# Products of a constant on TensorE, written to unused PSUM banks, at the beginning and at two joints of a six-stage decoder kernel

## The chip, the cores and the metric

The kernel runs on one core of one Trainium2 chip. The metric is the device time of one execution in microseconds (us). A core has five engines with queues of their own: TensorE (matrix products, shown as PE, its weight loads as PEld), VectorE (DVE), ScalarE (ACT), GpSimd (POOL) and SyncE (SP), which issues the DMAs here. They wait for each other by semaphores. TensorE writes only to PSUM, which has eight banks. TensorE's clock has two levels, 1.2 and 2.4 GHz; the profile shows which one was granted, as 0.50 and 1.00 of full speed.

## The reference

Two decoder layers over 32 sequences of 128 tokens with 256 features, all in float32. Each layer is self-attention, cross-attention and a feed-forward part, each with a layer norm before it and a residual add behind it:

```python
    x = x + _L0_attn_ref(_layernorm(x, axis=-1), L0_attn_Wqkv, L0_attn_bqkv, L0_attn_Wout, L0_attn_bout)
    x = x + _L0_xattn_ref(_layernorm(x, axis=-1), ctx_1024, L0_xattn_Wq, L0_xattn_bq, L0_xattn_Wk, L0_xattn_bk, L0_xattn_Wv, L0_xattn_bv, L0_xattn_We, L0_xattn_be)
    x = x + _L0_ffn_ref(_layernorm(x, axis=-1), L0_ffn_gate_W, L0_ffn_gate_b, L0_ffn_wi_W, L0_ffn_wi_b, L0_ffn_wo_W, L0_ffn_wo_b, L0_ffn_lora_A, L0_ffn_lora_B)
    x = x + _L1_attn_ref(_layernorm(x, axis=-1), L1_attn_W_query, L1_attn_W_key, L1_attn_W_val, L1_attn_W_out)
    x = x + _L1_xattn_ref(_layernorm(x, axis=-1), ctx_1024, ctx_1024, mask_SxS2_bk0, L1_xattn_wq, L1_xattn_bq, L1_xattn_wk, L1_xattn_bk, L1_xattn_wv, L1_xattn_bv, L1_xattn_wo, L1_xattn_bo)
    x = x + _L1_ffn_ref(_layernorm(x, axis=-1), L1_ffn_W_fc, L1_ffn_ln_w, L1_ffn_ln_b, L1_ffn_W_proj)
    return x
```

The first part is rotary attention with 16 heads of 16 features. The second mixes queries and keys of the context in one tanh layer and attends with one head. The third chooses one of eight experts for a token and adds its low-rank term (rank 4) to a shared feed-forward of 1024. The change touches the first three parts only.

## The kernel before

The activations (`x_res`) stay in SBUF for the whole kernel. The 32 sequences are worked on in 16 pairs (`NG` = 16 groups of `TOK` = 256 tokens). Each of the six parts is a stage, and each stage is a block of instructions for every engine: a0, b0, c0, a1, a2, d1. In the trace their tiles are called a_ (all three attention stages), b_, c_ and d_, and those shared by stages all_. A stage begins on an engine when all engines have ended the stage before.

In a stage the groups are pipelined in software: the order of each engine's instructions is written out by hand as a loop over windows, the first and last few unrolled. A window holds, for TensorE, steps of several groups. To keep float32 accuracy, most products run as three passes (`three_pass`, line 104: high part by high part, low by high, high by low) over operands that ScalarE rounds to a high part and from which VectorE or GpSimd takes the low part.

The places that matter here:

- **Beginning of stage a0.** SyncE loads the activations and weights. VectorE makes the constants (`Constants.prepare`; `ones` is one of them, line 129), normalises group 0 (`all_xn`), TensorE turns it (line 206, `a_FB<-all_ident,all_xn`), then waits until the weights are split (`all_odd_split`, line 298) and projects the queries (`a_FA`), the keys (`a_FB`) and the values (`a_FA`), then the value bias (line 1164). VectorE takes them out (`a_q`, line 901) and adds the bias of the values (line 996); with that the scores start (line 1010).
- **End of a0.** The last products are the output projection `a_FA` (line 104). VectorE adds it to `x_res` and splits the last of the next stage's weights (`all_even_split`, line 471). The score banks are `S1_0`, `S1_1`, `S2_0`, `S2_1`.
- **Beginning of b0.** ScalarE and GpSimd make the high and low part of the context (`b_cT_hi`, line 234; `b_cT_lo`, line 238). TensorE waits for both, then `b_ENT` has 24 products.
- **End of b0.** In the last window TensorE makes the last scores (`b_SC`, line 1444), waits for their exponentials (`b_probs`, line 1369, after two steps of VectorE), turns them (`b_PP`, line 1470) and multiplies with the values (`b_OUT`, line 1484).
- **Beginning of c0.** The gate (`c_RT`, 40 columns wide, line 104) is followed by the choice of the expert on VectorE (lines 1602 to 1611), and TensorE waits for its result `c_low_parts` before it turns it (`c_LT`, line 1692) and starts the hidden layer (`c_HB`, lines 1671 to 1674).

The order in the window of c0 at the place of the last edit is:

```python
                elif in_stage(w + 1):
                    gate(w + 1, 1 - parity)
                if in_stage(w - 1):
                    pe.wait_ge(hlo_ok, w * HALVES)
...
                if in_stage(w + 1):
                    pe.wait_ge(low_ok, w + 2)
```

Of the kernel before, what the change touches and what calls it, by code (L numbers as in the profile page):

```python
# [21 lines left out]
P = 128  # L22
# [4 lines left out]
NG = NB // PAIR  # L27
# [80 lines left out]
class Constants:  # L108


    def __init__(self, nm, a):
        self.from_dram = {k: a[k] for k in ("ident", "head_mask", "turn_sign")}
        self.tiles = {
            "ident": nm.sb("ident", [P, P]), "head_mask": nm.sb("head_mask", [P, HV]), "turn_sign": nm.sb("turn_sign", [P, 1]),
            "ones": nm.sb("ones", [P, P]), "minus_half": nm.sb("minus_half", [P, PAIR]), "minus_one": nm.sb("minus_one", [P, PAIR]), "ln_eps": nm.sb("ln_eps", [P, PAIR]),
            "ident_b": nm.sb("ident_b", [P, P], BF16), "neg_ident_b": nm.sb("neg_ident_b", [P, P], BF16),
        }
        self.loaded, self.ready = nm.sem("consts_loaded"), nm.sem("consts_ready")

    def load(self, sp):  # L120
        for k, src in self.from_dram.items():
# [2 lines left out]
    def prepare(self, dve):  # L124
        tiles = self.tiles
        dve.memset(tiles["minus_half"][:], -0.5)
        dve.memset(tiles["minus_one"][:], -1.0)
        dve.memset(tiles["ln_eps"][:], LN_EPS)
        dve.memset(tiles["ones"][:], 1.0)
        dve.wait_ge(self.loaded, 16 * len(self.from_dram))  # L130
        dve.tensor_copy(tiles["ident_b"][:], tiles["ident"][:])
        dve.tensor_scalar(tiles["neg_ident_b"][:], tiles["ident"][:], -1.0, None, ALU.mult).then_inc(self.ready, 1)


class GroupNorm:
# [434 lines left out]
def attention_stage(nc, name, before, norm, next_norm, consts, wt, following, spare, context=None, next_context=None, mask_dram=None,  # L570
# [90 lines left out]
    def has_window(G):  # L661
        return not isinstance(G, int) or G + 1 < NG
# [33 lines left out]
    with nc.Block() as block:  # L696
# [307 lines left out]
        def _(pe):  # L1004
# [176 lines left out]
            def group(G, parity):  # L1181
                for t in range(0, STEPS, 2):
                    if vo_bias and t == 0 and isinstance(G, int) and G == 0:
                        pe.wait_ge(vo_added, PAIR)
                    scores(G, t, parity)
                    if cross and has_step(G, t):
                        mask_step(G, t)
                        mask_step(G, t + 1)
                    if has_step(G, t - 2):
                        shift_step(G, t - 2)  # L1190
                        shift_step(G, t - 1)
                    if t in (0, 4) and whole(G - 1):
                        turn((G - 1) * PAIR + t // 4, t // 4)
                    if t in (2, 6) and whole(G - 1):
                        turn_back((G - 1) * PAIR + t // 4, t // 4)
                    if t == 0 and whole(G - 2):
                        output(G - 2)
                    if t == 0:
                        transposes(G)
                    if t == 2 and has_window(G):  # L1200
                        queries(G, parity)
                    if t == 4 and has_window(G):
                        keys(G)
                    if t == 6 and has_window(G):
                        values(G)
                    if vo_bias and t == 6 and isinstance(G, int) and G < 0:
                        value_bias()
                    if t == 6 and isinstance(G, int) and G == NG:
                        output(G - 1)
                    if t in (2, 6) and has_step(G, t - 6):  # L1210
                        for u in range(NQ):
                            av_step(G, t - 6 + u, parity)
                    if isinstance(G, int) and G >= following.first:
                        free = ((next_norm.lo_ok, 1), (max_ok, NG * STEPS)) if G + 1 >= NG else ((q_free, q_reads * (G + 2)),)
                        for u in range(2):
                            following.pe_slot(pe, (G - following.first) * STEPS + t + u, next_banks(G), free)
            if x_dram is not None:
                pe.wait_ge(constants.ready, 1)
            schedule(pe, group)
    nm.end()  # L1220
    return nm

# [71 lines left out]
def starts(w):  # L1294

    return isinstance(w, int) and w == 0
# [12 lines left out]
def in_stage(w):  # L1309
    return not isinstance(w, int) or 0 <= w < NG  # L1310


def entangled_stage(nc, name, before, norm, next_norm, consts, context, wt, following):
# [23 lines left out]
    with nc.Block() as block:  # L1337
# [99 lines left out]
        def _(pe):  # L1437
            def window(w, parity):
                if in_stage(w - 1):
                    pe.wait_ge(vt_ok, w)  # L1440
                    at_least(pe, exp_ok, w - 1)
                    for b in range(PAIR):
                        for k in range(KC):
                            last = pe.matmul(SC[:, b * P:(b + 1) * P], ent[:, k, b * P:(b + 1) * P],
                                             vT[:, k, b * P:(b + 1) * P], start=(k == 0), stop=(k == KC - 1))
                    last.then_inc(sc_full, 1)
                if not starts(w):
                    ln.pe_transpose(pe, w)
                if in_stage(w):
                    hi, lo, chi, clo = ln.hi[parity], ln.lo[parity], cT_hi[parity], cT_lo[parity]  # L1450
                    if isinstance(w, int) and w == 0:
                        pe.wait_ge(wt.w_ok, 3)
                    pe.wait_ge(ln.lo_ok, w + 1)
                    pe.wait_ge(c_lo, w + 1)
                    at_least(pe, ent_ok, w)
# [43 lines left out]
def routed_stage(nc, name, before, norm, next_norm, consts, wt, following):  # L1499
# [32 lines left out]
    with nc.Block() as block:  # L1532
# [109 lines left out]
        def _(pe):  # L1642
# [12 lines left out]
            def window(w, parity):  # L1655
# [19 lines left out]
                        last.then_inc(hb_full, 1)  # L1675
                elif in_stage(w + 1):
                    gate(w + 1, 1 - parity)
                if in_stage(w - 1):
                    pe.wait_ge(hlo_ok, w * HALVES)
                    at_least(pe, out_ok, w - 1)  # L1680
# [405 lines left out]
```

## Time and profile before

| | |
|---|---|
| median of 3 runs | 1392.95 us (1390.52 to 1396.66) |
| profiled execution, its time | 1392.18 us |
| its span (first to last instruction) | 1390.1 us |
| TensorE busy | 1318.4 us (95%) |
| mean granted clock of TensorE | 0.986 |
| VectorE, ScalarE, GpSimd busy | 71%, 53%, 33% |

The profile was taken from one execution. Its times start at the first instruction. An engine is busy while an instruction of it runs. A busy TensorE may run at either clock, so its busy time alone does not tell how fast it works.

### The profile page before, as it was taken

To read this page: it belongs to the slowest core of one execution; us is meant where nothing else is said; L and a number is where in the kernel's file an instruction comes from. 1 tells how busy PE (TensorE), PEld (TensorE's weight loads), DVE (VectorE), ACT (ScalarE), POOL (GpSimd) and SP (SyncE) were. 2 spreads that over 40 slices of the span, in tenths; PEclk is the share of its full clock that TensorE was granted. 3 is DMA by queue.
4 is the path that set the end of the run, shared out by engine and by line. 5 is a ranking of instruction groups with operands and counts; after the bars stand their busy time and mean duration, and the time that the engine had idled before them with its cause. 6 is when DMAs were issued, how large, how long until landed. Compare 5 with 4: busy or idle time off the path is not lost. (4 is left out here: it accounts for less than half of the span.)

```text
span 1390.1 us, 41799 instructions
## 1 busy us (share of the span) xinstructions
PE 1318.4 (95%) x15764; PEld 1192.3 (86%) x15764; DVE 987.4 (71%) x2431; ACT 732.8 (53%) x1469; POOL 455.0 (33%) x550
## 2 busy tenths in 40 slices
PE   5999999889978999999999999979999999899997
PEld 5899989789968999999899899868888888689997
DVE  5888888556655554554777778767777778768885
ACT  3655555445554544543556556535555556456562
POOL 2212221122221121210000000036555556478884
PEclk9999999999998999999999999999999999999999
DMA  6000000031100000000100000020000000000000
GB/s 233 2 2 0 0 0 2 2 113 38 38 4 28 2 0 0 0 0 3 54 2 0 0 0 1 2 78 17 17 15 15 15 15 2 2 24 23 30 31 31
DMA packets 16622, 29.26 MB, mean 21 GB/s; under 512 B 3632, under 2 KB 7728, under 8 KB 16144
## 3 DMA queue, kind: packets, MB, share of 16 engines
q1 hardware_dynamic: 16528, 27.97, 6.1%
q8 instruction: 64, 1.05, 0.3%
q14 instruction: 30, 0.25, 0.1%
HBM read 23.77 MB, written 4.19 MB: 20 GB/s over the span
## 5 line engine op out<-in xcount | busy, mean ns | idle before, releaser
L883 DVE TENSOR_REDUCE a_row_max<-a_S 128x4 bf16<-128x512 f32 (+1 forms) x384 | 247.1, 684 | 51.0 <-PE a_S L1051 25.5
L776 ACT ACTIVATE a_probs<-a_S 128x512 f32<-128x512 f32 x384 | 209.1, 595 | 117.2 <-PE a_S L1064 60.1
L175 POOL TENSOR_TENSOR all_var_eps<-all_moments,all_ln_eps 128x2 f32<-128x2 f32 x96 | 25.0, 260 | 604.8 <-DVE all_moments L170 604.8
L1019 PE MATMUL a_S<-a_qm_hi,all_odd_split 32*128 32x256 f32 x1536 | 188.5, 303 | 7.4 <-DVE a_row_max L883 5.6
L738 POOL TENSOR_TENSOR a_shifts<-a_add_mask,a_row_max 128x512 bf16<-128x512 bf16 x128 | 135.1, 1071 | 117.1 <-DVE a_row_max L883 117.1
L1019 PEld LDWEIGHTS a_S<-a_qm_hi,all_odd_split 32*128 32x128 f32 x1536 | 132.3, 184 | 41.8 <-issue 26.6
L1010 PE MATMUL a_S<-all_odd_split,a_qm_hi 32*128 32x128 f32 x1536 | 127.8, 285 | 1.7 <-DVE all_odd_weights L996 1.7
L1019 PE MATMUL a_S<-a_qm_lo,all_odd_split 32*128 32x256 f32 x768 | 108.8, 277 | 0.0
L1077 PE MATMUL a_AV<-a_probs,a_v_pad 128*32 128x128 f32 x3072 | 103.8, 276 | 0.0
L1010 PEld LDWEIGHTS a_S<-all_odd_split,a_qm_hi 32*128 32x128 f32 x1536 | 100.7, 186 | 2.7 <-DVE all_odd_weights L996 2.5
L781 ACT ACTIVATE a_av_raw<-a_AV 128x512 f32<-128x512 f32 x96 | 57.6, 600 | 77.0 <-PE a_AV L1077 76.1
L198 DVE TENSOR_SCALAR all_xn<-all_x_res,all_moments,all_rstd 128x256 f32 (+1 forms) x164 | 85.3, 561 | 14.1 <-POOL all_rstd L177 13.3
L104 PE MATMUL c_OUT<-all_odd_split,c_h_hi 128*128 128x256 f32 x512 | 90.3, 277 | 0.9 <-DVE all_x_res L1635 0.9
L1077 PEld LDWEIGHTS a_AV<-a_probs,a_v_pad 128*32 128x32 f32 x3072 | 78.0, 109 | 13.1 <-issue 1.5
L1769 POOL TENSOR_TENSOR d_scaled_hid<-d_hid,all_odd_weights 128x512 f32<-128x512 f32 x64 | 81.5, 1293 | 7.3 <-ACT d_hid L1801 6.3
L104 PE MATMUL a_FA<-all_odd_split 128*128 128x256 f32 x576 | 80.5, 289 | 2.0 <-DVE all_odd_split L896 1.9
L1566 ACT ACTIVATE c_h<-c_HB,all_odd_weights 128x256 f32<-128x256 f32 x128 | 53.8, 472 | 50.0 <-PE c_HB L1674 48.9
L1064 PE MATMUL a_S<-all_neg_ident_b,a_row_max 128*128 128x128 bf16 x1024 | 79.8, 221 | 0.0
L104 PEld LDWEIGHTS c_OUT<-all_odd_split,c_h_hi 128*128 128x128 f32 x512 | 78.5, 188 | 1.0 <-issue 1.0
L896 DVE TENSOR_TENSOR all_odd_split<-a_AV,all_odd_split 128x256 fp32r<-128x256 f32 x96 | 40.7, 424 | 51.3 <-ACT all_odd_split L786 50.4
L177 POOL TENSOR_TENSOR all_rstd<-all_var_eps,all_minus_half 128x2 f32<-128x2 f32 x96 | 73.2, 762 | 7.5
L104 PEld LDWEIGHTS a_FA<-all_odd_split 128*128 128x128 f32 x576 | 71.7, 190 | 2.6 <-DVE all_odd_split L896 2.3
(260 smaller groups left out, 3835.1 us busy)
## 6 DMA issues: line engine op xcount, KB each, us to landing
all_x_res<-in_x SPq DMA_DIRECT2D x8, 512.0 KB, 8.1
all_cx<-in_ctx_turned SPq DMA_DIRECT2D x16, 256.0 KB, 2.8
all_cx<-in_ctx SPq DMA_DIRECT2D x16, 256.0 KB, 2.8
out_x<-all_x_res SPq DMA_DIRECT2D x16, 256.0 KB, 2.0
b_routed_wi<-in_L_ffn_wi_W SPq DMA_DIRECT2D x1, 1024.0 KB, 5.1
b_routed_wo<-in_L_ffn_wo_W SPq DMA_DIRECT2D x1, 1024.0 KB, 7.4
all_even_weights<-in_L_ffn_W_fc SPq DMA_DIRECT2D x1, 1024.0 KB, 5.1
all_even_weights<-in_L_ffn_W_proj SPq DMA_DIRECT2D x1, 1024.0 KB, 6.9
```

The source lines that it names most:

```text
L104: last = pe.matmul(out, w(k), m(k), start=(k == 0 and n == 0), stop=(k == chunks - 1 and n == 2))
L177: pool.tensor_tensor(self.rstd[:], self.var_eps[:], self.minus_half[:], ALU.pow).then_inc(self.rstd_ok, 1)
L198: last = dve.tensor_scalar(self.xn[:, b, :], self.x(w, b), self.moments[:, b, 0:1], self.rstd[:, b:b + 1], ALU.subtract, ALU.mult)
L738: pool.tensor_tensor(shifts[:, t % 4], add_mask[:], row_max[:, t % 4, :].rearrange("p (h o) -> p h o", o=1).to_broadcast([P, QH, P]), ALU. ...
L776: act.activation(probs[:, t % STEPS, :], S2[t % 2][:], ACT.Exp, scale=DH ** -0.5).then_inc(exp_ok, 1)
L781: act.activation(av_raw[:], AV[b][:], ACT.Copy).then_inc(raw_ok, 1)
L883: dve.tensor_reduce(row_max[:, t % 4, :], S1[t % 2][:].rearrange("p (h k) -> p h k", h=QH), AXX, ALU.max).then_inc(max_ok, 1)
L1010: return pe.matmul(S1[t % 2][:, at * P:(at + 1) * P], qm_hi[parity][strip, c, b, v, :], k_hi[parity][strip, c, tok], start=(not cross or a ...
L1019: pe.matmul(S2[t % 2][:, c * HV * P:(c + 1) * HV * P], k[par][strip, c, tok], q[par][strip, c, b].rearrange("p h t -> p (h t)"), start=(c ...
L1064: last = pe.matmul(part, row_max[:, t % 4, h:h + 1].to_broadcast([P, P]), neg_ident_b[:], start=False, stop=h == QH - 1, skip_group_check= ...
L1077: last = pe.matmul(AV[b][32 * h:32 * h + 32, j * P:(j + 1) * P], v_pad[par][:, b, j * QH + h, :], probs[:, t % STEPS, h * P:(h + 1) * P], ...
L1769: pool.tensor_tensor(half_of(scaled_hid[parity], n), half_of(hid[parity], n), gain_row[:, half * HB_COLS:(half + 1) * HB_COLS], ALU.mult). ...
```

## The change

A helper `fill` issues a number of float32 products of the 128x128 tile of ones with itself, all to the first 128 columns of a PSUM bank that nothing is using at that point; nobody reads the result. It is called at six places in the code, and six groups of products come of it: 20 before the first wait for the constants, 18 behind the first transposes, 10 at the end of stage a0, 8 at the beginning of b0 before its first products, 14 in the last window of b0 and 10 behind the first gate of c0. A new semaphore tells TensorE that the ones are written.

```diff
-        self.loaded, self.ready = nm.sem("consts_loaded"), nm.sem("consts_ready")
+        self.loaded, self.ready, self.ones_ok = nm.sem("consts_loaded"), nm.sem("consts_ready"), nm.sem("ones_ok")
...
-        dve.memset(tiles["ones"][:], 1.0)
+        dve.memset(tiles["ones"][:], 1.0).then_inc(self.ones_ok, 1)
...
+def fill(pe, consts, bank, n):
+
+    for _ in range(n):
+        pe.matmul(bank[:, 0:P], consts["ones"][:], consts["ones"][:], start=True, stop=True, skip_group_check=True)
...
                     if t == 2 and has_window(G):
+                        if x_dram is not None and isinstance(G, int) and G < 0:
+                            fill(pe, consts, S2[0], 18)
                         queries(G, parity)
...
             if x_dram is not None:
+                pe.wait_ge(constants.ones_ok, 1)
+                fill(pe, consts, S2[0], 20)
                 pe.wait_ge(constants.ready, 1)
             schedule(pe, group)
+            if x_dram is not None:
+                fill(pe, consts, S2[0], 10)
...
+                if isinstance(w, int) and w == NG:
+                    fill(pe, consts, VT, 14)
                 if not starts(w):
                     ln.pe_transpose(pe, w)
...
                     if isinstance(w, int) and w == 0:
                         pe.wait_ge(wt.w_ok, 3)
+                        fill(pe, consts, VTOK, 8)
                     pe.wait_ge(ln.lo_ok, w + 1)
...
                 elif in_stage(w + 1):
                     gate(w + 1, 1 - parity)
+                    fill(pe, consts, OUT, 10)
```

TensorE's queue at the start of the kernel, first as it was (a_FB takes the turned group 0, a_FA the queries):

```order
L1003 UNCONDITIONAL_BRANCH
L206 MATMUL a_FB<-all_ident,all_xn 128x128 x4
L104 MATMUL a_FA<-all_xT_hi,all_odd_split 128x256 x2
L104 MATMUL a_FA<-all_xT_lo,all_odd_split 128x256
L104 MATMUL a_FA<-all_xT_hi,all_odd_split 128x256 x2
```

and as it is in the changed kernel (its lines are numbered a little higher):

```order
L1009 UNCONDITIONAL_BRANCH
L138 MATMUL a_S_0<-all_ones 128x128 x20
L212 MATMUL a_FB<-all_ident,all_xn 128x128 x4
L138 MATMUL a_S_0<-all_ones 128x128 x18
L104 MATMUL a_FA<-all_xT_hi,all_odd_split 128x256 x2
L104 MATMUL a_FA<-all_xT_lo,all_odd_split 128x256
```

Both groups stand ahead of instructions that wait, so these can start only when the products of ones are through. TensorE's queue across the end of b0 and the start of c0 (the two branches are the stage's end and start), in the changed kernel:

```order
L1506 MATMUL b_VTOK<-all_ident,b_vT 128x128 x4
L1456 MATMUL b_SC<-b_vT,b_ent 128x128 x4
L138 MATMUL b_VT<-all_ones 128x128 x14
L1485 MATMUL b_PP<-all_ident,b_probs 128x128 x2
L1499 MATMUL b_OUT<-b_v_tok,b_probsT 128x256 x2
L1349 UNCONDITIONAL_BRANCH
L1656 UNCONDITIONAL_BRANCH
L104 MATMUL c_RT<-all_odd_split,all_xT_hi 128x40
...
L138 MATMUL c_OUT<-all_ones 128x128 x10
L1708 MATMUL c_LT<-all_ident,c_low_parts 96x128 x2
L212 MATMUL c_PT<-all_ident,all_xn 128x128 x4
```

Before, the same rows stood there without the two of line 138. Nothing else moved, on TensorE or on another engine.

## Rows read from the trace of the kernel before

**Rows 1.** The page: TensorE's busy time and the granted clock in 40 slices

```profile
PE 1318.4 (95%) x15764; PEld 1192.3 (86%) x15764; DVE 987.4 (71%) x2431; ACT 732.8 (53%) x1469; POOL 455.0 (33%) x550
...
PEclk9999999999998999999999999999999999999999
```

**Rows 2.** TensorE by stretch: length, busy (records), granted clock, DMA share, GB/s

```profile
14.67:18.63 3.96, 3.93 (x18) 1.00 1.02 415
18.63:25.46 6.83, 5.23 (x40) 1.00 1.03 358
25.46:32.28 6.82, 6.78 (x60) 0.50 0.06 20
282.32:288.28 5.96, 5.93 (x28) 0.50 0.97 382
411.16:424.82 13.66, 9.17 (x37) 0.50 0.26 79
420.56:424.82 4.26, 4.26 (x20) 0.50 0.01 4
435.06:438.47 3.41, 3.41 (x18) 0.50 0.00 0
```

**Rows 3.** Timeline at a0's end and b0's start: start, us, engine, instruction [idle before]

```profile
275.64 1.70 PE L104 MATMUL a_FA<-all_odd_split 128*128 128x256 f32 x12 [0.93 <-DVE all_odd_split L896]
...
279.25 0.68 DVE L471 TENSOR_TENSOR all_even_split<-all_even_weights,all_even_split 128x512 fp32r<-128x512 f32 x1
...
280.94 1.26 POOL L238 TENSOR_TENSOR b_cT_lo<-all_cx,b_cT_hi 128x512 fp32r<-128x512 f32 x1 [21.60 <-ACT b_cT_hi L234]
...
282.35 0.77 PE L104 MATMUL b_ENT<-all_xT_hi,all_even_split 128*128 128x256 f32 x2 [5.01 <-POOL b_cT_lo L238]
```

**Rows 4.** Waits of TensorE: us in total, times, longest

```profile
PE a_FB L206 <- DVE all_xn L198: 8.7, 1, 8.7
...
PE c_LT L1692 <- DVE c_low_parts L1611: 4.7, 2, 2.6
```

**Rows 5.** Timeline at the beginning of a0

```profile
0.94 0.17 DVE L129 MEMSET all_ones<- 128x128 f32 x1
...
8.65 1.09 PE L206 MATMUL a_FB<-all_ident,all_xn 128*128 128x128 f32 x4 [8.65 <-DVE all_xn L198]
...
14.70 0.77 PE L104 MATMUL a_FA<-all_xT_hi,all_odd_split 128*128 128x256 f32 x2 [4.96 <-DVE all_odd_split L298]
...
17.71 0.88 DVE L901 SCALAR_TENSOR_TENSOR a_q<-a_FA,all_odd_weights 128x256 f32<-128x256 f32 x2 [1.95 <-PE a_FA L104]
...
22.65 0.75 DVE L996 TENSOR_TENSOR all_odd_weights<-all_odd_weights,a_S 128x256 f32<-128x256 f32 x2 [0.34 <-PE a_S L1164]
...
23.46 0.66 PE L1010 MATMUL a_S<-all_odd_split,a_qm_hi 32*128 32x128 f32 x8 [0.84 <-DVE all_odd_weights L996]
...
25.50 0.58 PE L1019 MATMUL a_S<-a_qm_hi,all_odd_split 32*128 32x256 f32 x2 [0.79 <-DVE a_row_max L883]
```

**Rows 6.** Timeline of TensorE at b0's end and c0's start

```profile
404.71 1.02 PE L1484 MATMUL b_OUT<-b_v_tok,b_probsT 128*128 128x256 f32 x4
405.80 0.66 PE L1491 MATMUL b_VTOK<-all_ident,b_vT 128*128 128x128 f32 x4
406.29 1.06 PE L1444 MATMUL b_SC<-b_vT,b_ent 128*128 128x128 f32 x8
410.83 0.44 PE L1470 MATMUL b_PP<-all_ident,b_probs 128*128 128x128 f32 x2 [3.48 <-ACT b_probs L1369]
411.74 2.07 PE L1484 MATMUL b_OUT<-b_v_tok,b_probsT 128*128 128x256 f32 x4 [0.47 <-ACT b_probsT L1379]
415.27 0.37 PE L104 MATMUL c_RT<-all_odd_split,all_xT_hi 128*128 128x40 f32 x1 [1.46 <-PEq L1337]
...
417.62 0.38 PE L104 MATMUL c_RT<-all_odd_split,all_xT_hi 128*128 128x40 f32 x1
```

**Rows 7.** TensorE by shape, 404 to 408 us: count | busy, mean ns | idle

```profile
L1444 PE MATMUL b_SC<-b_vT,b_ent 128*128 128x128 f32 x8 | 1.1, 275 | 0.0
```

## What the change was predicted to do

> **What bounds the kernel now.** I read the page first: TensorE is busy 95% of the span, so where its stream gets faster or stops waiting, the kernel is likely to gain. Of the slices of the granted clock only one is below 9 [rows 1]. Then the same clock by stretch [rows 2]: it is at half (1.2 instead of 2.4 GHz) from 25.46 to 32.28 us, 282.32 to 288.28 (where it had work), 411.16 to 424.82 and 435.06 to 438.47. Before 18.63 the view has no record and prints 1.00, but the pace tells the level: 18 records in 3.96 us are 0.22 us each, as 28 in 5.96 us (0.21) are at half clock, while twelve products of the same 256 columns took 1.70 us, 0.14 each, at full clock [rows 3]. So the products from 14.67 to 18.63 ran at half clock too. Last the waits of TensorE [rows 4] and the timeline around them [rows 3, 5, 6]: each of these stretches but two follows one of the long waits into which the change puts products: 8.65 and 4.96 us at the beginning, 5.01 at the joint of stages a and b, 3.48 and 2.56 around the joint of b and c.
>
> **The price of one product of ones.** Nearest row: the b_SC products are also float32, 128x128 on both sides. Four products are eight records in the trace and take 1.06 us [rows 6]; with 0.28 for the last (the mean of one [rows 7]), the other seven take 0.78, 0.11 a record, **0.22 us a product at full clock**. At half clock it is twice that: the b_OUT products took 1.02 us at full and 2.07 at half [rows 6]. So 0.43 us. The bounds of the price are these two, since the clock has two levels. Nothing waits for a fill's result; its cost is lateness of what stands behind it on TensorE alone.
>
> **The beginning.** The ones are there at 1.11 us (0.94 + 0.17), the first transposes start at 8.65 [rows 5]: 7.5 us of cover. Twenty products at half clock are 8.6 us; but the clock rose 3.96, 4.26, 5.96 and 6.82 us after dense work began (at 14.67, 420.56, 282.32, 25.46) [rows 2]. With a rise after 5.5 us (I take the middle of these), 13 products are done by 6.6 us and the other 7 take 1.5: 8.2 us, just in time. With a rise after 6.8 they end at about 8.9, 0.2 late. Then the transposes (1.09 us at half clock [rows 5], 0.66 for four at full [rows 6]) end about 0.4 earlier, and 18 products at full clock, 4.0 us, lie in the wait of 4.96. So queries, keys and the start of the values run at full clock: 3.96 us of work become 1.98. Who uses it? VectorE takes the queries at 17.71 and would find them about 1.6 earlier; its queue up to the bias of the values at 22.65 is a chain of such steps behind TensorE, and the scores at 23.46 wait for it [rows 5]. I take **1.8 us** (0.2 from earlier transposes, 1.6 from this chain); bounds 0 and 2.2.
> The stretch from 25.46 to 32.28 stays: no fill stands in it, and the waits that precede it (0.84 and 0.79 us [rows 5]) are dependencies through VectorE.
>
> **The joint of a and b.** The 12 products of a_FA end at 277.34; ten fills end at 279.6. Stage a ends when VectorE has split the weights, 279.93 (279.25 + 0.68), so they are covered [rows 3]; without that cover they would cost up to 2.2. Eight fills from about 280.3 take 1.8, to 282.1. GpSimd is done with b_cT_lo at 282.20, and the first b_ENT product starts at 282.35 [rows 3]: no delay, at most 0.2. The wait of 5.01 us shrinks to pieces of at most 0.7, the clock stays up, and the 5.96 us from 282.32 to 288.28 become 2.98 [rows 2]. ScalarE and VectorE wait for these products, so the start of b's pipeline moves with them. **2.9 us**; bounds 0 and 3.1.
>
> **The joint of b and c.** Fourteen fills take 3.1 us of the 3.48 that TensorE waits for the last b_probs; then b_OUT takes 1.02 instead of 2.07, and the end of stage b and the start of c come **1.0 us** earlier [rows 6]. What follows is uncertain. After b_OUT TensorE has nothing for some 1.4 us, until the gate products c_RT, which have only 40 columns; they now start at about 414.2. If the clock falls again there, the gates take their 2.7 us as before, and the ten fills start at 416.9 at half clock: 4.3 us against 2.6 of cover [rows 6, 4], 1.7 late. In return the clock, given dense work from 416.9 and not only from 420.56 less 1.0, rises about 1 to 3 us earlier, and the products of c_HB start nearly at full clock instead of running 4.26 us at half [rows 2]: about 1.7 back. Net of this joint: **1.0**. If it doesn't fall, the gates take 1.3 instead of 2.7, the ten fills 2.2 of 2.6 us, and the 4.26 us become 2.13: 1.0 + 1.3 + 2.1 = **4.4**.
> Which? By the rows it can fall after short waits: it fell at 25.46 though the last 6.83 us had 5.23 busy and no wait above 0.84 [rows 2, 5], and at 435.06 after one of 2.1 us [rows 4]. I take the fall.
> The Trainium skill ("TensorE: Matmul & The Clock Gate", the table of "Why this matters for your kernels") asks only that no idle gap between bursts exceed about 3 us. By that rule the gap of 1.4 us would do no harm and this joint would give 4.4; this trace does not agree with it at 25.46 and 435.06, so it is a rival and not the forecast. The same page ("A second HAM failure mode: psum-queue depth-cycling") says that frequent short idles alone can make the clock go down and up, which would leave the 1.0.
>
> **Sum.** 1.8 + 2.9 + 1.0 = 5.7 us. The profiled execution took 1392.18 us (span 1390.1, 2.1 around it), 0.8 below the median of 1392.95. 1392.2 - 5.7 = **1386.5 us**. The other queues get nothing but one semaphore increment on VectorE's memset. A measurement of this kernel can tell about 0.5%, 7 us, from no change; the sum is just below that.
>
> **Rivals.**
> 1. *The clock holds through the joint of b and c* (above): 1.8 + 2.9 + 4.4 = 9.1, 1383.1 us. For it: only 0.5 and 1.4 us idle in the way, and the fills before are dense. Against it: the two falls named. Chance 0.28.
> 2. *The clock moves, the chain does not, or it falls elsewhere.* The stretches at half clock may come back one group later (as at 25.46), or VectorE, ScalarE or DMA take over: at the beginning the weights' split is ready at its own time, and in c the route on VectorE is 2.56 us whatever the clock. Then the joint of a and b gives its 2.9 or part of it and little else: 1 to 3 us, 1390 us. Chance 0.22.
> 3. *Slower: products of ones do not hold the clock up*, or cost 0.43 each. From the covers the turning point is 0.25 us a product: 18 in 4.96 us plus what the transposes save, 14 in 3.48, 10 in 2.56 with a hand-over. At 0.43: the first twenty end at 9.7, 1.0 late, the eighteen push the queries to 18.5, 3.7 late in all; at a/b the ten end at 281.6, 1.7 late, and the eight 1.3 more; the fourteen are 2.5 late, the last ten 1.7. Together 10.9: 1403 us. Against it: b_SC, the same shape at the same place, ran at 0.22, and the clock is up at both joints when the fills begin. Chance 0.05.
> The forecast itself has 0.45.
>
> **How the numbers follow.** Each term of the forecast may be off by a microsecond or so: its own range is 1384 to 1389. Rival 1 has 1381.5 to 1385.5, rival 2 up to 1392. The range 1382 to 1390.5 leaves out the slower case, a part of rival 2 and the far end of rival 1, some 2 in 10. Faster by over 0.5% means below 1386.0: nearly all of rival 1 (0.26) and somewhat less than half of the forecast (0.19): 0.45. Slower by over 0.5% is rival 3, 0.05. The rest, 0.50, is within 0.5%.
>
> **What would show it.** Beginning: the fills at 0.43 us at first and 0.22 later, a full clock some 4 to 7 us after 1.1, the transposes at 8.6 to 8.9, 18 fills before 13.5, products of a_FA 0.11 us apart from the first, the scores at about 21.7 instead of 23.46. Joint a/b: full clock all through, b_ENT starting within 0.3 us of POOL's b_cT_lo, its 24 products in under 3 us. Joint b/c: b_PP directly after b_probs, b_OUT in 1.0 us; then either half clock from about 414 to 421 with c_LT late behind the fills, or full clock throughout. Wrong would be: a fill over 0.25 us at full clock, b_ENT or c_LT held by fills, or a new stretch at half clock right behind a joint.

## The result and the profile after

| | before | changed |
|---|---|---|
| median | 1392.95 us, 7 runs (1390.52 to 1396.66) | 1383.56 us, 7 runs (1382.35 to 1388.88) |
| profiled execution, its time | 1392.18 us | 1382.35 us |
| its span | 1390.1 us | 1380.2 us |
| mean granted clock | 0.986 | 0.994 |

The ratio of the times is 0.9943, with a 95% interval of 0.9924 to 0.9961: 7.9 us less, 5.4 to 10.6. The forecast was 1386.5 us in a range from 1382 to 1390.5.

The changed kernel's seven executions fall into two clusters: 1382.35 to 1383.56 us with a mean clock of 0.994 (four), and 1386.06 to 1388.88 with 0.988 or 0.989 (three). The same program thus differs by up to 6.5 us, and the clock goes with it. The profiled execution is the fastest of the seven, so the profile shows the better case.

The page of the changed kernel, the two lines that answer to [rows 1]:

```profile
PE 1328.9 (96%) x15924; PEld 1204.0 (87%) x15924; DVE 985.0 (71%) x2431; ACT 732.0 (53%) x1469; POOL 455.1 (33%) x550
...
PEclk9999999999999999999999999999999999999999
```

TensorE is busy 10.5 us longer, in 160 more records, and the span is 9.9 us shorter. The 160 records are the 80 products, two records each. The clock by stretch (length, busy (records), granted clock, DMA share, GB/s), which answers to [rows 2], up to 902.73 us:

```profile
5.02:271.26 266.24, 258.55 (x3932) 1.00 0.08 29
271.26:274.68 3.42, 2.94 (x14) 0.50 0.00 0
274.68:411.21 136.53, 128.72 (x1010) 1.00 0.16 49
411.21:414.62 3.41, 3.41 (x18) 0.50 0.68 231
414.62:902.73 488.11, 475.98 (x5776) 1.00 0.02 5
```

Before, the first 500 us had four stretches at half clock, 30.7 us together, beside the products up to 18.63. Now there are two, 6.8 us. The one in group 0 and the one around 435 us, which the forecast left in place, did not come in this execution; a new one stands at 271.26, ahead of the joint of a and b.

TensorE's timeline at the three places (start, us; the bracket is the idle time before), for [rows 5]:

```profile
1.16 6.57 PE L138 MATMUL a_S<-all_ones 128*128 128x128 f32 x40 [1.16 <-DVE all_ones L129]
9.35 0.63 PE L212 MATMUL a_FB<-all_ident,all_xn 128*128 128x128 f32 x4 [1.63 <-DVE all_xn L204]
9.82 4.18 PE L138 MATMUL a_S<-all_ones 128*128 128x128 f32 x36
14.95 0.47 PE L104 MATMUL a_FA<-all_xT_hi,all_odd_split 128*128 128x256 f32 x2 [0.94 <-DVE all_odd_split L304]
...
22.03 0.66 PE L1016 MATMUL a_S<-all_odd_split,a_qm_hi 32*128 32x128 f32 x8 [0.88 <-DVE all_odd_weights L1002]
```

for [rows 3]:

```profile
271.74 2.93 PE L104 MATMUL a_FA<-all_odd_split 128*128 128x256 f32 x12 [0.93 <-DVE all_odd_split L902]
274.46 2.50 PE L138 MATMUL a_S<-all_ones 128*128 128x128 f32 x20
277.58 2.02 PE L138 MATMUL b_VTOK<-all_ones 128*128 128x128 f32 x16 [0.61 <-PEq L702]
279.68 0.47 PE L104 MATMUL b_ENT<-all_xT_hi,all_even_split 128*128 128x256 f32 x2
```

and for [rows 6]:

```profile
402.02 3.29 PE L138 MATMUL b_VT<-all_ones 128*128 128x128 f32 x28
405.67 0.44 PE L1485 MATMUL b_PP<-all_ident,b_probs 128*128 128x128 f32 x2 [0.35 <-ACT b_probs L1381]
406.58 1.13 PE L1499 MATMUL b_OUT<-b_v_tok,b_probsT 128*128 128x256 f32 x4 [0.47 <-ACT b_probsT L1391]
409.17 0.26 PE L104 MATMUL c_RT<-all_odd_split,all_xT_hi 128*128 128x40 f32 x1 [1.46 <-PEq L1349]
...
410.50 3.97 PE L138 MATMUL c_OUT<-all_ones 128*128 128x128 f32 x20
414.26 0.57 PE L1708 MATMUL c_LT<-all_ident,c_low_parts 128*96 128x128 f32 x2
```

What to see: the eighteen fills take 4.18 us for 36 records (0.12 a record with the last one's tail, so 0.22 to 0.23 a product). The clock's record begins at 5.02; the pace tells that it rose there: 18 records of the first twenty products stand in the 3.86 us before, 0.21 each, and the rest take 2.71 us, 0.12 each. So more than half of them ran at full clock. The waits of 8.65, 4.96, 5.01 and 3.48 us are down to 1.63, 0.94, 0.61 and 0.35. But the last ten take 3.97 us, because the clock fell 0.7 us after they began.

Where the 9.9 us of the profiled pair come from, by the start of the same work in both:

| work | before | changed | earlier by |
|---|---|---|---|
| first scores of group 0 | 23.46 | 22.03 | 1.4 |
| a0's output projection | 275.64 | 271.74 | 3.9 |
| b_ENT | 282.35 | 279.68 | 2.7 |
| last b_PP | 410.83 | 405.67 | 5.2 |
| first c_RT | 415.27 | 409.17 | 6.1 |
| c_LT | 420.56 | 414.26 | 6.3 |
| second gate of c0 (c_RT) | 428.23 | 420.51 | 7.7 |
| a c_HB behind the stretch at 435 us | 439.09 | 429.84 | 9.3 |
| end of the span | 1390.1 | 1380.2 | 9.9 |

Read step by step, 1.4 us come from the beginning, 1.3 from the joint of a and b (3.9 to 5.2) and 2.6 from the joint of b and c (5.2 to 7.7): 5.3 at the places with fills. Another 4.0 us come where no fill stands: 2.5 in group 0 and 1.5 at 435 us, because two stretches at half clock did not come in this execution. The last 0.6 us are gained later.

### The profile page after: what moved, and what is told of

The parts are those of the page before. It is cut to its first block and busy times, and to the rows that moved or that the text cites. A ratio compares the mean times of both kernels' runs of the same rounds, so it can differ in the third digit from the quotient of the medians.

```text
span 1380.2 us, 42119 instructions
## 1 busy us (share of the span) xinstructions
PE 1328.9 (96%) x15924; PEld 1204.0 (87%) x15924; DVE 985.0 (71%) x2431; ACT 732.0 (53%) x1469; POOL 455.1 (33%) x550
## 5 line engine op out<-in xcount | busy, mean ns | idle before, releaser
L204 DVE TENSOR_SCALAR all_xn<-all_x_res,all_moments,all_rstd 128x256 f32 (+1 forms) x164 | 84.3, 555 | 14.9 <-POOL all_rstd L183 14.2
```

Source lines behind the costliest of these rows:

```text
L204: last = dve.tensor_scalar(self.xn[:, b, :], self.x(w, b), self.moments[:, b, 0:1], self.rstd[:, b:b + 1], ALU.subtract, ALU.mult)
```

## The experiments

Ratios are to the kernel before, timed beside each experiment (its medians were 1391.6 to 1393.0 us), with their 95% intervals. A per mille of the time is 1.4 us, and two experiments within about 2 us of each other are hardly told apart. Each kernel has one profile. Where a text says how far a kernel is ahead, the start of the same product is compared with that in the profile of the kernel before.

### Each place alone

Each takes fills out of the change (with the conditions that stand above them): e1 keeps those of the beginning, e2 those of the joint of a and b, e3 those of the joint of b and c:

```diff
e1
-                fill(pe, consts, S2[0], 10)
-                        fill(pe, consts, VTOK, 8)
-                    fill(pe, consts, VT, 14)
-                    fill(pe, consts, OUT, 10)
e2
-                            fill(pe, consts, S2[0], 18)
-                fill(pe, consts, S2[0], 20)
-                    fill(pe, consts, VT, 14)
-                    fill(pe, consts, OUT, 10)
e3
-                            fill(pe, consts, S2[0], 18)
-                fill(pe, consts, S2[0], 20)
-                fill(pe, consts, S2[0], 10)
-                        fill(pe, consts, VTOK, 8)
```

> Only the 20 and 18 products at the beginning stay. The prediction's own theory (each place gives what its own wait hides): the scores start about 1.4 to 2.0 us earlier, the stretch at half clock in group 0 (25.46 to 32.28 before) stays, and the time falls by 1.8 us. Rival (the early products also spare later falls): the stretch in group 0 does not come, about 3 us more, so 4.4 to 4.8 us in all. Third theory (such a fall comes or stays away from execution to execution): a median between, 2 to 4.5 us.

> Only the 10 products at the end of a0 and the 8 at the beginning of b0 stay. The prediction's theory: the 24 products of b_ENT run at full clock, 2.9 us gained. Rival (the output projection of a0, just before, falls to half clock as it did in the profile of the change): 1.2 us of it are given back, 1.6 gained. The stretch of group 0 at half clock should be in this profile.

> Only the 14 products at the end of b0 and the 10 behind the first gate of c0 stay. The prediction's theory: 1.0 us if the clock falls once more, 4.4 if it holds. Rival (it falls once more, but rises before c_HB, and the later stretch around 435 us does not come either): c_HB and what follows at full clock, 2.5 to 4.5 us gained although the ten are late by about 1 us.

| | median | ratio (interval) | us against before |
|---|---|---|---|
| e1, beginning | 1389.33 | 0.9979 (0.9967 to 0.9991) | 2.9 less |
| e2, joint a/b | 1391.44 | 0.9989 (0.9977 to 1.0001) | 1.5 less |
| e3, joint b/c | 1389.20 | 0.9973 (0.9959 to 0.9987) | 3.8 less |

The three add up to 8.2 us, against 7.9 for the change: additive, as far as a resolution of about 3 us for the sum can tell. The profiles show less at the places themselves: e1 is 2.1 us ahead behind its fills, e2 0.2 us from a0's projection to the last b_PP, and e3 1.3 us from the last b_PP to the second gate. The rest of the 8.2 us comes from stretches elsewhere that came or stayed away.

**e1.** The scores start at 21.39 us, 2.07 earlier, a little more than forecast. The group's stretch at half clock did come in this profile (length, busy, clock):

```profile
23.30:30.13 6.83, 6.70 (x60) 0.50 0.37 124
279.30:286.13 6.83, 5.86 (x27) 0.50 0.95 343
409.01:422.66 13.65, 9.13 (x36) 0.50 0.24 77
```

So the early products don't reliably spare it. The stretches begin 2.2 us before those of the kernel before [rows 2], as the work does (b_ENT at 280.27, 2.1 earlier). The lead of 2.1 us stays as it is to the end of the kernel (2.1 at 1385 us). The first theory (1.8 us) lies inside the interval of 1.3 to 4.6 us, and so does the third, that the stretch comes and goes; the rival of 4.4 and more is at its edge.

**e2.** The gain is about half of the forecast's 2.9 and not clear of nothing. TensorE, VectorE and GpSimd at the joint, in time order:

```profile
275.42 2.93 PE L104 MATMUL a_FA<-all_odd_split 128*128 128x256 f32 x12 [0.93 <-DVE all_odd_split L902]
278.15 3.97 PE L138 MATMUL a_S<-all_ones 128*128 128x128 f32 x20
282.41 0.75 DVE L173 BATCH_NORM_STATS2 all_stats<-all_x_res 128x6 f32<-128x256 f32 x2 [1.48 <-PEq L702]
282.41 2.02 PE L138 MATMUL b_VTOK<-all_ones 128*128 128x128 f32 x16 [0.30 <-PEq L702]
283.10 1.26 POOL L244 TENSOR_TENSOR b_cT_lo<-all_cx,b_cT_hi 128x512 fp32r<-128x512 f32 x1 [23.98 <-ACT b_cT_hi L240]
284.51 0.48 PE L104 MATMUL b_ENT<-all_xT_hi,all_even_split 128*128 128x256 f32 x2
```

The clock had fallen at 274.62, before the fills. a0's projection took 2.93 us instead of 1.70, and the ten fills 3.97 us: VectorE was through at 280.93 (280.25 + 0.68) and stood 1.48 us for the next stage, which before took 0.33. b_ENT starts 2.2 us later than in [rows 3] and runs at full clock; its end is where the two nearly cancel (b_VTOK at 290.69 against 291.21 before). Of the lateness, 1.2 us are the projection's own and 1.15 are that of the fills. The latter is what the slower rival named, at one place and in one execution: fills queued ahead of a stage's end while the clock is down.

**e3.** Almost four times the forecast's 1.0. In this profile the clock did what the prediction had taken: it fell at 413.38, ahead of the gates at 414.07, so gates and ten ran at half and c_LT came 6.56 us behind c_RT, at 420.63, no earlier than before. But it was back at 420.20, before c_HB, and the second gate starts at 426.70 instead of 428.23: 1.5 us, of which 0.3 were there before the fills (the last b_PP at 410.57). So the joint gave 1.3 us in the profile, where I had 1.0. The stretch around 435 us is missing too, 1.5 us more. The rival with 2.5 to 4.5 us fits the time; whether it is due to the fills that the last stretch is missing stays open, since it is missing in e2 as well, which has no fills there.

### The last ten products: none, or five

```diff
e4
-                    fill(pe, consts, OUT, 10)
e8
-                    fill(pe, consts, OUT, 10)
+                    fill(pe, consts, OUT, 5)
```

> The change without the last ten products (behind the first gate of c0). The prediction's theory says that they cost 1.7 us of lateness and give 1.7 back: same time as the change within 1 us. Rival (they are what raises the clock before c_HB): c_HB starts 1 us earlier but runs at half clock, 2.1 us, and 1 to 3 us slower than the change. If they only cost their lateness of 1.1 us: 1.1 us faster than the change.

> The change with 5 instead of 10 products behind the first gate of c0. If the ten are late by 1.1 us as in the profile of the change and five would do for the clock: 1.1 us faster than the change, about 8.5 to 9 us below before. If the number is what raises the clock in time: between the change and the change without them, 1 us slower than the change.

e4: median 1386.64, ratio 0.9959 (0.9945 to 0.9973), 2.2 us more than the change. e8: 1386.39, 0.9963 (0.9949 to 0.9976), 2.8 more. Both differences go the same way, but their intervals overlap that of the change, so the case rests on the traces too. From the first gate product to the second gate (c_RT to c_RT) it is 12.96 us before, 11.34 in the change, 12.19 in e4 and 11.62 in e8. In e4 the clock fell at 412.37, in the wait behind the gates; c_LT came after 2.56 us of wait, and c_HB began at half (0.2 us from one product to the next instead of 0.12):

```profile
413.88 0.66 PE L1707 MATMUL c_LT<-all_ident,c_low_parts 128*96 128x128 f32 x2 [2.56 <-DVE c_low_parts L1626]
415.17 0.55 PE L1686 MATMUL c_HB<-all_xT_hi,all_odd_split 128*128 128x256 f32 x1
415.52 0.42 PE L1687 MATMUL c_HB<-all_xT_hi,all_odd_split 128*128 128x256 f32 x1
415.74 0.41 PE L1688 MATMUL c_HB<-all_xT_lo,all_odd_split 128*128 128x256 f32 x1
```

So the ten delay c_LT by about 1.1 us (5.09 from c_RT against 4.04) and pay for it because c_HB is at full clock from its start. Whether five are better is open. In e8 the stretch lasted 6.82 us instead of 3.41, but it began at 408.74, ahead of the gates and so before the five were reached:

```profile
409.45 0.37 PE L104 MATMUL c_RT<-all_odd_split,all_xT_hi 128*128 128x40 f32 x1 [1.46 <-PEq L1349]
...
412.01 2.48 PE L138 MATMUL c_OUT<-all_ones 128*128 128x128 f32 x10
414.73 0.66 PE L1708 MATMUL c_LT<-all_ident,c_low_parts 128*96 128x128 f32 x2 [0.24 <-DVE c_low_parts L1626]
```

c_LT came 5.28 us behind c_RT because the gates ran at half clock; it waited 0.24 us for the route, and the five did not hold it. In e3 the clock had the same course with ten products, and from the first gate to the second it took 12.63 us, 1.0 more than e8. That e8's median lies above the change is in its profile the work of other places: the stretch in group 0 came, and two near 1180 and 1207 us cost it 1.5 us. In e4's profile the two near 1180 and 1207 us and the one around 435 us came too, so neither median is the price of the last ten alone.

### Twice as many of all

```diff
-                fill(pe, consts, S2[0], 20)
+                fill(pe, consts, S2[0], 40)
...
-                    fill(pe, consts, OUT, 10)
+                    fill(pe, consts, OUT, 20)
```

> All six groups twice as large (40, 36, 10 to 20, 8 to 16, 28, 20). If every product beyond the wait's length is lateness at 0.22 us: beginning 20 more x 0.22 - 1.6 = 2.8 and 18 more x 0.22 - 0.9 = 3.0, end of a0 10 more x 0.22 - 0.5 = 1.7, start of b0 1.8, end of b0 14 more x 0.22 - 0.35 = 2.7, c0 2.2: 14 us, so slower than before by about 5 us (1397 to 1399). If the clock's gain grows with more dense work (fewer falls): 3 to 4 us of it come back, 1393 to 1395. If a fill's lateness is absorbed behind other engines: under 5 us above the change, below 1390.

Median 1400.59, ratio 1.0072 (1.0058 to 1.0086): 10.0 us slower than before, 18 above the change by the ratios. The profile, whose span is 15.3 us longer than the change's, can be held against the 14 worked out. TensorE's timeline:

```profile
1.16 11.85 PE L138 MATMUL a_S<-all_ones 128*128 128x128 f32 x80 [1.16 <-DVE all_ones L129]
12.85 0.60 PE L212 MATMUL a_FB<-all_ident,all_xn 128*128 128x128 f32 x4
13.28 8.20 PE L138 MATMUL a_S<-all_ones 128*128 128x128 f32 x72
...
424.88 4.71 PE L138 MATMUL c_OUT<-all_ones 128*128 128x128 f32 x40
```

The scores start at 28.30, 6.3 us behind the change, where 5.8 were worked out. From a0's output projection (280.18) to b_ENT (291.56) it is 3.4 us more than in the change, 3.5 worked out. From b_VTOK (297.76) to the last b_PP (420.10) it is 2.5 more, 2.7 worked out. Only in c0 the twenty are cheaper than their 2.2: c_LT comes 5.88 us behind c_RT, 0.8 more than in the change, because the clock held there and twenty took 4.71 us where ten had taken 3.97. Products beyond a wait are paid nearly in full, and the clock gives little back; of the three theories the first, with 1397 to 1399 us, came nearest. The stretch ahead of the joint of a and b came all the same (276.41 to 283.24).

### The beginning without its first twenty

```diff
             if x_dram is not None:
                 pe.wait_ge(constants.ones_ok, 1)
-                fill(pe, consts, S2[0], 20)
                 pe.wait_ge(constants.ready, 1)
```

> The change without the first 20 products; the 18 behind the first transposes stay. The prediction's theory: the clock is at half when the 18 begin at 9.7 us, rises 4 to 6.8 us later, so they end at 15.5 to 17 instead of 13.9, up to 2 us behind the weights' split; the queries then run at full clock: 1 to 2 us slower than the change. Rival (the 18 alone do the warming and the lateness is hidden by the weights' DMA and VectorE): same as the change.

Median 1386.36, ratio 0.9955 (0.9940 to 0.9971): 1.7 us more than the change, as the first theory had it, though again inside the intervals. The eighteen begin at 9.64 and take 5.76 us for their 36 records instead of 4.18; the clock rose at 12.95, with the fills half through, and they end at 15.40. The first product of a_FA follows at 15.16 without a wait (the last records overlap); in e1, with transposes at the same time (8.72 against 8.76), it is at 14.31 after 0.95 us of wait. That is 0.85 us late, and the scores are 0.8 us behind those of e1. The twenty do two things: they start the warming early, and they keep the eighteen short.

### The short waits

The stretches that remained stand near waits of under 1 us. e6 adds fills in group 0, e7 in the last three waits of a0, e9 in the last window of b0; e10 has all three, e12 also eight in the second route.

```diff
e6
+                    early = x_dram is not None and isinstance(G, int) and G == 0
+                    if early and t in (0, 2):
+                        fill(pe, consts, S2[0], 3)
                     if vo_bias and t == 0 and isinstance(G, int) and G == 0:
e7
+                    ending = x_dram is not None and isinstance(G, int) and G == NG
+                    if ending and t in (4, 6):
+                        fill(pe, consts, S2[0], 3)
                     if t in (0, 4) and whole(G - 1):
...
                     if t == 6 and isinstance(G, int) and G == NG:
+                        if ending:
+                            fill(pe, consts, S2[0], 4)
                         output(G - 1)
e9
+                last_window = isinstance(w, int) and w == NG
+                if last_window:
+                    fill(pe, consts, VT, 2)
                 if in_stage(w - 1):
                     pe.wait_ge(pp_ok, w)
...
                     last.then_inc(out_full, 1)
+                if last_window:
+                    fill(pe, consts, VT, 4)
e12
+                if isinstance(w, int) and w == 0:
+                    fill(pe, consts, OUT, 8)
                 if in_stage(w + 1):
                     pe.wait_ge(low_ok, w + 2)
```

> The change and three products more in each of the two waits of group 0 (0.88 us before the first scores, 0.79 before the second ones); the stretch at half clock behind them was in the profiles of four of six kernels here. If the short waits are what lets the clock fall there: no such stretch in the profile, and the median falls by 1 to 3 us below the change's (3 us where it would have come). Rival (it falls because of work that fills little of the array, not because of the waits): the stretch stays in some executions, same time as the change.

> The change and 3, 3 and 4 products more in the last three waits of a0 (0.72, 0.88, 0.93 us). The a/b joint alone gave only 1.5 us; in its profile the clock fell at 274.62, ahead of its products, which then ran at half clock and ended stage a0 1.5 us late. If those waits cause it: the output projection in 1.7 us and no stretch at half clock from 265 to 290, 1 to 2 us below the change. Rival (the price of ten more products, hand-overs included, takes what the clock gives): same as the change within 0.5 us.

> The change and, in the last window of b0, 2 products more before b_OUT (wait of 0.47 us) and 4 behind it (VectorE needs 0.9 us there before the stage can end). A test of the prediction's first rival, that the clock holds through this joint: in every profile so far with the ten products in c0 it was at half for 3.4 us around them, and c_LT came 1.1 to 2.7 us late. If the short waits cause it: the ten take 2.2 to 2.5 us, c_LT comes 5.2 to 5.3 us behind c_RT's start less 1.1, about 1 us below the change. Rival (the 40-column gates and the 1.46 us without work between the stages are enough to let it fall): same as the change, or 0.3 slower.

> The change with the additions of group 0, of a0's tail and of b0's end together. If each spares a fall in a part of the executions: 2 to 4 us below the change, 1380 to 1382, and the spread of its runs narrower. If one fall spared only lets the next come: same as the change within 1 us.

> As e10, and 8 products more in the second wait for the chosen expert (2.15 us at about 432 in the kernel before; followed by a stretch of 3.4 us at half clock in four of the profiles so far). If that wait is what lets it fall: 0.5 to 1.7 us below e10. Rival: lateness of the 8 takes it back, same as e10.

| | median (runs) | ratio (interval) |
|---|---|---|
| change | 1383.56 (7) | 0.9943 (0.9924 to 0.9961) |
| e6, group 0 | 1383.31 (5) | 0.9941 (0.9928 to 0.9955) |
| e7, a0's tail | 1384.17 (5) | 0.9941 (0.9928 to 0.9955) |
| e9, b0's end | 1383.74 (7) | 0.9938 (0.9916 to 0.9960) |
| e10, all three | 1381.00 (6) | 0.9919 (0.9893 to 0.9945) |
| e12, and the second route | 1380.44 (6) | 0.9918 (0.9892 to 0.9944) |

Three counts in these expectations do not fit the profiles: the stretch in group 0 was in five of the first six (not four), the one around 435 us in five of the first ten (not four), and in e3, which has the ten in c0, the clock was down for 6.8 us around them and not for 3.4.

Alone, none is told apart from the change, so e6, e7 and e9 missed the 1 to 3 us that their first theories gave. In their profiles the stretch that each was aimed at is absent, but others came: in group 0 in e7, at 267.67 us in e9, around 435 us in e6 and e7, near 1180 and 1207 us in e6 and e9. Together they are the fastest: 11.3 us below before (7.7 to 14.9), within what was expected of e10. The intervals overlap that of the change, but five of e10's six executions and five of e12's six are below the fastest of the change's seven (1382.35). e12 is the same as e10, as its rival had it, though in its profile the stretch around 435 us is absent and in e10's it is there.

What the clock did at each place, over the profiles of all fourteen kernels, one profile each:

| place | fills in its short waits | without them |
|---|---|---|
| group 0, behind the first scores | none at half in 3 of 3 (e6, e10, e12) | at half in 8 of 11 |
| end of a0 to b0's start, with the 18 fills there | none in 3 of 3 (e7, e10, e12) | at half in 5 of 8 |
| joint of b and c, with the last ten | none in 3 of 3 (e9, e10, e12) | at half in 5 of 5 (e8 with five: at half; e5 with twenty: not) |

The cases of the middle column are few: e10 and e12 stand in all three rows. What the clock's course was worth at the two joints, by how far each profile gets ahead from one product to the next:

| from, to | clock | profiles | gained, us |
|---|---|---|---|
| a0's output projection to the last b_PP | full throughout | e4, e6, e7, e8, e10, e12 | 2.1 to 2.6 |
| the same | fell ahead of the joint | changed, e2, e9, e11 | 0.0 to 1.3 |
| last b_PP to the second gate of c0 | full throughout | e9, e10, e12 | 3.7 to 3.8 |
| the same, ten products | fell in the gates or the ten | changed, e6, e7, e11 | 2.5 to 2.7 |
| the same, ten products | fell ahead of the gates | e3 | 1.3 |
| the same, five products | fell ahead of the gates | e8 | 2.3 |
| the same, none in c0 | fell behind the gates | e4 | 1.7 |

Whether the waits themselves let the clock fall is not shown. In e5, e9 and e11 it fell before a0's end only 0.56, 0.26 and 0.55 us into the first of the three short waits. e9, where it fell at 267.67:

```profile
264.28 1.84 PE L457 MATMUL a_S<-all_even_weights 128*128 128x1 f32 x16
265.99 0.42 PE L1096 MATMUL a_AV<-all_ident,a_o_tok 128*128 128x128 f32 x2
266.33 1.08 PE L1083 MATMUL a_AV<-a_probs,a_v_pad 128*32 128x128 f32 x32
268.13 1.12 PE L1090 MATMUL a_AV<-all_ident,a_av_raw 128*128 128x128 f32 x4 [0.72 <-ACT a_av_raw L787]
```

From 255.00 to 267.67 TensorE was busy 12.41 of 12.67 us, the last of it with products of one column (128x1) and products with 32 of 128 columns of weights (128*32). That is the rival in the expectation of e6: work that fills little of the array. The added products are full ones and shorten the waits at once, so these experiments do not tell the two apart.

e9 shows the joint of b and c as the prediction's first rival wanted it (TensorE in time order):

```profile
407.16 0.61 PE L138 MATMUL b_VT<-all_ones 128*128 128x128 f32 x4
407.80 1.13 PE L1502 MATMUL b_OUT<-b_v_tok,b_probsT 128*128 128x256 f32 x4
408.76 1.05 PE L138 MATMUL b_VT<-all_ones 128*128 128x128 f32 x8
410.39 0.26 PE L104 MATMUL c_RT<-all_odd_split,all_xT_hi 128*128 128x40 f32 x1 [0.57 <-PEq L1349]
...
411.72 2.48 PE L138 MATMUL c_OUT<-all_ones 128*128 128x128 f32 x20
414.43 0.42 PE L1713 MATMUL c_LT<-all_ident,c_low_parts 128*96 128x128 f32 x2 [0.24 <-DVE c_low_parts L1631]
```

The ten take 2.48 us, TensorE waits 0.24 for the route, and c_LT comes 4.04 us behind c_RT instead of 5.09; c_RT to the second gate is 10.15 us instead of 11.34. The six fills of e9 sit in time in which other engines were working (ScalarE ahead of b_OUT, VectorE behind it), so they cost nothing: from b_PP to c_RT it is 3.51 us, 3.50 in the change. But e9's own time did not fall by this 1.2 us, and its profile shows one thing against it: the clock was at half from 267.67 to 277.90, 10.2 us, at the joint before. e12's clock record up to 1369 us, where it falls once more:

```profile
7.08:915.03 907.95, 883.10 (x10877) 1.00 0.07 21
915.03:918.44 3.41, 3.41 (x27) 0.50 0.00 0
918.44:1369.00 450.56, 428.72 (x4989) 1.00 0.06 18
```

## Why the prediction came out as it did

The time, 1383.56 us, lies in the range, and below the forecast of 1386.5; the measured gain of 7.9 us (5.4 to 10.6) stands against 5.7. The mechanism was the one described: products of ones in a wait bring the clock up or hold it, and the work behind runs at full clock. The sum was in part luck. In the profiles the places with fills gave 5.3 us, near the 5.7, but as 1.4, 1.3 and 2.6 and not as 1.8, 2.9 and 1.0: two terms were off in opposite directions. Most of the rest of the 9.9 us came from two stretches that I had left in place. One of the signs that I had named as wrong did come: c_LT was held by the fills. Step by step:

- **The price of a fill** was right: 0.22 to 0.23 us at full clock, and up to 3.97 us for ten at half, 0.40 each with the edges.
- **The beginning, 1.8 us:** e1 gives 2.9 (1.3 to 4.6). The clock rose 3.9 us after the first fill in the changed kernel (3.7 to 5.9 in the others that have it). Scores came 1.4 us earlier, although the first transposes started 0.7 later for another reason: VectorE's first wait, for a DMA of the constants, ended at 6.00 instead of 5.29. In e1, without that, 2.1. My note that the stretch in group 0 "stays: no fill stands in it" was half right: it came in e1, e4, e5, e7 and e8, and not in the changed kernel, e9 and e11, none of which has a fill there. Where it stayed away, as in the changed kernel, it gave 2.5 us that the forecast did not have.
- **The joint of a and b, 2.9 us:** e2 gives 1.5 (-0.1 to 3.2). The term is mis-sized because it took the clock to be up when the joint begins. In the changed kernel, e2, e5, e9 and e11 it fell earlier, during the short waits of 0.72, 0.88 and 0.93 us at the end of a0. In the changed kernel that made the output projection 1.2 us longer, and b_ENT, 3.9 us ahead before it, only 2.7 ahead. In the profiles in which the clock stayed up, the joint gave 2.1 to 2.6 us, near the term.
- **The joint of b and c, 1.0 us:** the other mis-sized term. I had the clock fall ahead of the gates, the gates at half and c_LT 1.7 us late. In the changed kernel the gates ran at full clock, the fall came 0.7 us into the ten, they were 1.1 us late, and the clock was back before c_HB. This gives 0.94 us (b_PP to c_RT) and 1.62 (c_RT to the second gate), 2.6 in all. In e3 the fall did come ahead of the gates, and there the joint gave 1.3 us, near the term; e3's time fell by more, 3.8 (1.8 to 5.7), of which the absent stretch at 435 us is 1.5. The stretch at 435 us, which I had left in place, was absent in both; it was there in 6 of the 14 profiles.
- **Rivals.** That the clock holds through the joint of b and c did not happen, but e9, e10 and e12 show that it can be had with six more products: then the joint gave 3.7 to 3.8 us, against the 4.4 of the rival. The second rival's case (1 to 3 us in all) is out. The slower one decides nothing for the change, yet its mechanism is real where the clock is down when the fills are reached (e2), and where there are too many (e5).
- **Short waits.** The clock fell at 271.26 in the changed kernel with no wait above 0.93 us near it, and at 267.67 in e9 with 0.26 us idle in the 12.67 us before. With products in the short waits no fall came at those places in nine of nine cases; without them it came in 18 of 24. The Trainium skill ("TensorE: Matmul & The Clock Gate", "Why this matters for your kernels") asks for no idle gap above about 3 us between bursts of products. These traces do not agree that this is enough to keep the clock up.

Open: which of the remaining stretches (around 902 to 927, 1180 to 1220 and 1370 us) come with the change and which come anyway. The profiles of e2, e3, e4, e6, e8 and e9 all have stretches near 1180 and 1207 us that neither the kernel before nor the change shows; they cost these profiles 1.3 to 3.1 us. They were not studied. Nor did any run put products of ones where TensorE has no wait and the clock is up, or full products in the place of the light ones at a0's end, which would tell the waits from the light work.

## What to carry to other kernels

Look for waits of TensorE with no dependency on its own result, price one dummy product from a row of the same shape at either clock, and put in no more than fit: here up to the wait they returned about 8 us of 1393, and twice as many cost 10. The short waits ahead of a long one may be worth filling too: with the clock already down when the fills are reached, e2 was left with 0.2 us at that joint, and with it up other profiles had 2.1 to 2.6. Judge such a change by several executions and by the clock of each, since one program varied by up to 6.5 us with the stretches that happened to come.

## What was not expected of the hardware

- TensorE's clock can fall without a long wait: near waits of 0.84 and 0.79 us in group 0, and at a0's end in the last of waits of 0.72, 0.88 and 0.93 us, with TensorE busy 1.21 of the 3.20 us before (changed kernel, 268.00 to 271.20).
- It can fall with hardly a wait: in e9 TensorE was busy 12.41 of 12.67 us before, at last with products of one column and with 32 columns of weights.
- The same program does not get the same clock in every execution: mean clocks of 0.988 to 0.994 in seven runs of the changed kernel, and with them 1382 to 1389 us.
- Float32 products of ones that nobody reads raise the clock as real work does: it rose at 5.02 us, 3.9 us after the first twenty began, and in e11 at 12.95, 3.3 us after the eighteen began.
